# First feed-forward: the attention sum's shift by one token moved from TensorE to the sync queue's transfers

## The reference, cut to what matters

```python
def shift_token(t):                      # the second half of the channels comes from the token before
    t1, t2 = jnp.split(t, 2, axis=-1)
    t2 = jnp.pad(t2, ((0, 0), (1, 0), (0, 0)))[:, :-1]
    return jnp.concatenate([t1, t2], axis=-1)

def _layer(x, ...):
    ...                                  # local attention, 8 heads of 64, windows of 128 tokens, gives o
    x = x + o @ wo
    h = shift_token(x)
    mu = h.mean(-1, keepdims=True)
    var = h.var(-1, keepdims=True)
    h = (h - mu) / jnp.sqrt(var + 1e-05) * lg + lb
    h = h @ w1 + b1
    a, g = jnp.split(h, 2, axis=-1)
    h = a * jax.nn.gelu(g, approximate=False)
    x = x + h @ w2 + b2
    return x
```

## Time and profile before

| what | value |
|---|---|
| runs | 1794.33, 1794.79, 1800.66 us; median 1794.79 |
| the profiled execution's own time | 1796.17 us |
| its span in the trace | 1794.3 us |
| mean granted TensorE clock | 0.893 of full speed |
| busy PE / DVE / ACT / POOL | 83% / 60% / 41% / 24% of the span |
| the stage that the change is in | about 190 to 951 us |

### The profile page before, as it was taken

The page is one execution under the profiler, slowest core; times in us unless marked ns, Lnnn a source line. Parts: engine busy times, 40 slices in busy tenths (PEclk is TensorE's granted clock), DMA queues, the critical chain, the costliest instruction groups (busy, mean ns, idle before and its releaser), DMA issues. The chain is left out here.

```text
span 1794.3 us, 31159 instructions
## 1 busy us (share of the span) xinstructions
PE 1486.6 (83%) x9550; PEld 1171.4 (65%) x9551; DVE 1068.5 (60%) x2885; ACT 743.3 (41%) x1784; POOL 437.1 (24%) x469
## 2 busy tenths in 40 slices
PE   4985799999999999999998887299265699729992
PEld 3762477777777777777776565288142388618992
DVE  3326666666667777777765642677777566552223
ACT  1211555555556655555553211055266234202330
POOL 2102222222222222333321146111321100036321
PEclk9978899999999999999996798599675699859997
DMA  6001000000000000000003343610100000112104
GB/s 239 0 1 55 1 1 2 0 0 1 0 4 22 33 2 0 0 0 0 1 1 140 129 150 118 241 84 0 36 1 0 3 1 0 47 40 82 49 31 146
DMA packets 27138, 74.60 MB, mean 42 GB/s; under 512 B 6587, under 2 KB 11853, under 8 KB 25004
## 3 DMA queue, kind: packets, MB, share of 16 engines
q1 hardware_dynamic: 20236, 55.44, 8.3%
q0 software_dynamic: 6816, 18.14, 3.3%
HBM read 54.22 MB, written 20.88 MB: 42 GB/s over the span
## 5 line engine op out<-in xcount | busy, mean ns | idle before, releaser
L1124 PE MATMUL banks<-l_ffn_h2T,l_ffn_w 128*128 128x128 f32 (+1 forms) x1536 | 193.4, 277 | 0.0
L1124 PEld LDWEIGHTS banks<-l_ffn_h2T,l_ffn_w 128*128 128x128 f32 (+1 forms) x1536 | 178.6, 179 | 11.1 <-issue 5.7
L1041 PE MATMUL banks<-l_ffn_in_wqkv,l_ffn_hT 128*128 128x512 f32 x384 | 182.2, 612 | 0.8 <-ACT l_ffn_hT L1201 0.8
L1223 ACT ACTIVATE l_ffn_work<-l_ffn_work,l_ffn_att_bias 128x256 f32<-128x256 f32 x256 | 126.4, 495 | 76.9 <-DVE l_ffn_att_bias L1365 76.9
L1251 ACT ACTIVATE l_ffn_gate<-banks,l_ffn_layer_cols 128x128 f32<-128x128 f32 x192 | 59.9, 362 | 200.9 <-PE banks L1124 187.7
L1041 PEld LDWEIGHTS banks<-l_ffn_in_wqkv,l_ffn_hT 128*128 128x128 f32 x384 | 69.4, 194 | 75.8 <-issue 74.6
L265 POOL TENSOR_TENSOR rstd<-mean_var,neg_half 128x1 f32 x64 | 35.2, 550 | 338.3 <-DVE mean_var L258 338.3
L1132 PE MATMUL banks<-l_ffn_in_w,l_ffn_ff 128*128 128x256 f32 (+1 forms) x384 | 107.8, 396 | 0.0
L990 POOL TENSOR_TENSOR l_ffn_rden_wide<-l_ffn_att_rden,ones 128x512 f32<-128x512 f32 x32 | 33.3, 1040 | 273.1 <-DVE l_ffn_att_rden L1376 273.1
L2175 DVE COPY l_plan_c_all<-l_ffn_in_w 128x1024 f32 x39 | 31.4, 806 | 101.7 <-PE banks L2109 89.4
L1257 ACT ACT_TABLE_LOAD x68 | 87.2, 1283 | 1.2
(11 more groups left out here) (408 smaller groups left out, 3500.1 us busy)
## 6 DMA issues: line engine op xcount, KB each, us to landing
l_plan_rows<-l_plan_pairs SPq DMA_DIRECT2D x16, 512.0 KB, 8.3
l_ffn_in_w<-in_L_w SPq DMA_DIRECT2D x2, 4096.0 KB, 21.1
l_ffn_in_down<-in_L_down SPq DMA_DIRECT2D x1, 4096.0 KB, 14.4
l_plan_pairs<-l_plan_rows SPq DMA_DIRECT2D x4, 1024.0 KB, 7.0
l_plan_table<-l_plan_rows SPq DMA_DIRECT2D x8, 512.0 KB, 2.8
l_ffn_in_wqkv<-in_L_wqkv SPq DMA_DIRECT2D x1, 3072.0 KB, 12.1
l_ffn_w<-in_L_w SPq DMA_DIRECT2D x2, 1364.0 KB, 7.3
x_res<-in_x SPq DMA_DIRECT2D x4, 512.0 KB, 5.4
```

The costliest lines, as they stand in the source:

```text
L1041: mm = pe.matmul(ps[:, (Q, K, V)[n], :], hT[:, m.b, m.odd, ch, 1 - ch:P + 1 - ch], wqkv[:, bass.ds(m.layer, 1), ch, n * INNER:(n + 1) * IN ...
L1124: mm = pe.matmul(ps[0:FW[j], HIDDEN[pair], to:to + P], w1[:, ch, at:at + FW[j]], h2T[:, ch, m.b, :], start=(j % 2, n, ch) == (0, 0, 0), st ...
L1223: ex = nc.scalar.activation(work[:, m.b, slot, :], work[:, m.b, slot, :], ACT.Exp, bias=bias[:, m.b, slot:slot + 1], scale=-1.0, accum_out ...
```

## The change: what it does

`shifted` and its two products leave TensorE, and the two 128x128 matrices that it used are no longer loaded. In their place SyncE runs a step per item: it waits for y1 of the item and issues two transfers inside SBUF, each of the upper 128 channels in f32: one of 127 rows (partitions 0 to 126 to partitions 1 to 127), one of a single row (partition 127 of the tile before to partition 0). Both add 16 to the new semaphore `row_moved`, so that an item is done at 32. VectorE reads the shifted half from the new SBUF tile `moved` instead of PSUM. In VectorE's step, `shifted_stats` is split: `own_stats` stays, `moved_stats` stands after `take_y(after)`, and `normalise_h2` stands after `gated(old, 2)`. The two loads of the second layer are woven into SyncE's steps. LIFT, the offset of all semaphore counts, goes from 16 to 128.

```diff
-LIFT = 16
+LIFT = 128
...
-        self.shift = sb("shift", [P, 2, P])
...
+        moved = sb("moved", [P, BATCH, D - P])
...
             @block.sync
             def _(sp):
-                with sp.Fori(1, LAYERS) as layer:
-                    first = layer * HALF
-                    sp.wait_ge(s.rot_ready.sem, s.rot_ready.at(first, 0))
+                def move_row(m):
+                    sp.wait_ge(s.y1_ready.sem, s.y1_ready.at(m.turn, m.k))
+                    sp.dma_start(moved[1:P, m.b, :], y1[0:P - 1, m.b, m.odd, P:D]).then_inc(s.row_moved.sem, 16)
+                    sp.dma_start(moved[0:1, m.b, :], y1[P - 1:P, m.b, 1 - m.odd, P:D]).then_inc(s.row_moved.sem, 16)
...
+                def step(old, now, new, after):
+                    if now and new and new.opens and new.q == 0:
+                        next_rotation(new.layer)
+                    if now:
+                        move_row(now)
+                    if old and now and now.opens and now.q == 0:
+                        next_up(now.layer)
...
-                def shifted(m):
-                    pe.wait_ge(s.y1_ready.sem, s.y1_ready.at(m.turn, m.k))
-                    pe.matmul(ps[:, SHIFTED, D:D + P], shift[:, 0, :], y1[:, m.b, m.odd, P:D], start=True, stop=False)
-                    pe.matmul(ps[:, SHIFTED, D:D + P], shift[:, 1, :], y1[:, m.b, 1 - m.odd, P:D], start=False, stop=True)\
-                      .then_inc(s.shift_psum.sem, 1)
...
                     if old:
                         ffn_up(old, 1)
-                    if now:
-                        shifted(now)
-                    if old:
                         ffn_up(old, 2)
...
-                def shifted_stats(m):
+                def own_stats(m):
                     v.wait_ge(s.y1_ready.sem, s.y1_ready.at(m.turn, m.k))
                     v.bn_stats(bn2[:, m.b, 0, :], y1[:, m.b, m.odd, 0:P])
-                    v.wait_ge(s.shift_psum.sem, s.shift_psum.at(m.turn, m.k))
-                    dve.link(v.bn_stats(bn2[:, m.b, 1, :], ps[:, SHIFTED, D:D + P]))
+
+                def moved_stats(m):
+                    v.wait_ge(s.row_moved.sem, s.row_moved.at(m.turn, MOVED * m.k))
+                    dve.link(v.bn_stats(bn2[:, m.b, 1, :], moved[:, m.b, :]))
...
-                    v.tensor_scalar(h2[:, m.b, P:D], ps[:, SHIFTED, D:D + P], mv2[:, m.b, 0:1], rstd2[:, m.b:m.b + 1], ALU.subtract, ALU.mult)\
+                    v.tensor_scalar(h2[:, m.b, P:D], moved[:, m.b, :], mv2[:, m.b, 0:1], rstd2[:, m.b:m.b + 1], ALU.subtract, ALU.mult)\
...
                     if now:
                         add_attention(now)
-                        shifted_stats(now)
+                        own_stats(now)
                     if old:
                         gated(old, 1)
                     if after:
                         take_y(after)
                     if now:
-                        normalise_h2(now)
+                        moved_stats(now)
                     if old:
                         gated(old, 2)
+                    if now:
+                        normalise_h2(now)
                     if old and old.closes and old.q > 0:
                         stats_of(old.i, old.q - 1)
```

More of the change, by code:

```diff
@@ L126, in __init__ @@
         self.y1_ready = new("y1_ready")
-        self.shift_psum = new("shift_psum")
+        self.row_moved = new("row_moved")
         self.shift_var = new("shift_var")
@@ L213, in build @@
         e.s, e.dma_sem = Signals(new), sem
-        e.chain = {n: Chain(sem(f"{n}_order")) for n in ("dve", "act", "pool", "pe")}
+        e.chain = {n: Chain(sem(f"{n}_order")) for n in ("dve", "act", "pool", "pe", "sp")}
         e.loaded = sem("loaded")
@@ L405, in __init__ @@
         self.qk_scale = sb("qk_scale", [P, LAYERS, 2, 2, DH])
-        self.shift = sb("shift", [P, 2, P])
         self.mask32 = sb("mask32", [P, 3, 2 * P])
         super().__init__(e, "l0_ffn", ((self.all_cols, "L0_cols"), (self.all_b2, "L0_b2"), (self.qk_scale, "L0_qk_scale"),
-                         (self.shift, "shift"), (self.mask32, "mask"), (self.wqkv, "L0_wqkv"), (self.wo, "L0_wo"), (self.w2, "L0_w2")))
+                         (self.mask32, "mask"), (self.wqkv, "L0_wqkv"), (self.wo, "L0_wo"), (self.w2, "L0_w2")))
 class L0Xattn(Ahead):
@@ L822 @@
 HUGE = 3e38
+MOVED = 32
 def l0_ffn(e, ffn):
@@ L832, in l0_ffn @@
         sb = memory(e, ctx, "l0_ffn")
-        wqkv, wo, w2, all_cols, all_b2, qk_scale, shift, mask32 = (ffn.wqkv, ffn.wo, ffn.w2, ffn.all_cols, ffn.all_b2, ffn.qk_scale, ffn.shift, ffn.mask32)
+        wqkv, wo, w2, all_cols, all_b2, qk_scale, mask32 = (ffn.wqkv, ffn.wo, ffn.w2, ffn.all_cols, ffn.all_b2, ffn.qk_scale, ffn.mask32)
         y = sb("y", [P, ALL_TILES, D])
@@ L893, in l0_ffn @@
                 s.rot_ready, s.qkT_psum, s.qT_ready, s.kT_ready, s.rden_ready, s.rden_wide, s.mixed_psum, s.mix_ready, s.mixT_psum,
-                s.mixT_ready, s.out_psum, s.y1_ready, s.shift_psum, s.shift_var, s.shift_rstd, s.h2_ready, s.h2T_psum,
+                s.mixT_ready, s.out_psum, s.y1_ready, s.shift_var, s.shift_rstd, s.h2_ready, s.h2T_psum,
                 s.h2T_ready, s.y1b_ready, s.ffn_out, s.y_done)
@@ L900, in l0_ffn @@
         begin(4 * FPAIRS, s.hid_psum, s.gate_ready, s.ff_ready)
+        begin(4 * MOVED, s.row_moved)
         class Item:
@@ L913, in l0_ffn @@
         Q_T, K_T = 0, 1
-        SCORES, RDEN_T, MIXED, OUT, SHIFTED, H2_T = 2, 2, 3, 4, 4, 5
+        SCORES, RDEN_T, MIXED, OUT, H2_T = 2, 2, 3, 4, 5
         V, HIDDEN, DOWN, Y_T = 6, (6, 7, 6), 7, 3
@@ L958, in _, with next_rotation, next_up, first @@
             def _(sp):
-                with sp.Fori(1, LAYERS) as layer:
-                    first = layer * HALF
-                    sp.wait_ge(s.rot_ready.sem, s.rot_ready.at(first, 0))
+                def move_row(m):
+                    sp.wait_ge(s.y1_ready.sem, s.y1_ready.at(m.turn, m.k))
+                    sp.dma_start(moved[1:P, m.b, :], y1[0:P - 1, m.b, m.odd, P:D]).then_inc(s.row_moved.sem, 16)
+                    sp.dma_start(moved[0:1, m.b, :], y1[P - 1:P, m.b, 1 - m.odd, P:D]).then_inc(s.row_moved.sem, 16)
+                def next_rotation(layer):
+                    sp.wait_ge(s.rot_ready.sem, s.rot_ready.at(layer * HALF, 0))
                     sp.dma_start(rot[:], d["rotary"]).then_inc(rot_loaded, 16)
-                    sp.wait_ge(s.hid_psum.sem, s.hid_psum.at(first, 0))
+                def next_up(layer):
+                    sp.wait_ge(s.hid_psum.sem, s.hid_psum.at(layer * HALF, 0))
                     sp.dma_start(w1[:], d["L0_w1"][bass.ds(layer, 1)].rearrange("l p c n -> (l p) c n"))\
                       .then_inc(w1_loaded, 16)
+                def first(new):
+                    pass
+                def step(old, now, new, after):
[5 more added lines that the diff above has]
+                        next_up(now.layer)
+                layers(sp, e.chain["sp"], lambda layer: None, first, step)
             @block.gpsimd
@@ L1385, in add_attention @@
                     v.wait_ge(s.out_psum.sem, s.out_psum.at(m.turn, m.k))
-                    v.wait_ge(s.shift_psum.sem, s.shift_psum.at(m.turn, m.k - 2))
+                    v.wait_ge(s.h2_ready.sem, s.h2_ready.at(m.turn, m.k - 2))
                     v.wait_ge(s.y1b_ready.sem, s.y1b_ready.at(m.turn, m.k - 2))
                     if m.opens and m.q == 0:
-                        v.wait_ge(s.shift_psum.sem, s.shift_psum.at(m.turn, m.k - 1))
+                        v.wait_ge(s.row_moved.sem, s.row_moved.at(m.turn, MOVED * (m.k - 1)))
                         v.wait_ge(s.y1b_ready.sem, s.y1b_ready.at(m.turn, m.k - 1))
@@ L1480, in _ @@
                 layers(v, dve, lambda layer: None, first, step)
-        end(turns, *four, s.scores_psum, s.probs_ready, s.probsT_psum, s.bias_ready, s.pT_act, s.pT_dve, s.hid_psum, s.gate_ready, s.ff_ready)
+        end(turns, *four, s.row_moved, s.scores_psum, s.probs_ready, s.probsT_psum, s.bias_ready, s.pT_act, s.pT_dve, s.hid_psum, s.gate_ready, s.ff_ready)
         end(HALF, s.ln_var, s.ln_rstd)
```

## The result

The changed kernel takes 1851.8 us (median of 4 runs, 1848.6 to 1852.4) beside 1795.5 us for the kernel before on the same chip: 1.030 times as long, 95% interval 1.028 to 1.032. The forecast was 1858 us, with 1808 to 1930 as its range.

What follows compares the result with a forecast made beforehand. PE's order of work was taken to bound the first feed-forward stage. Waits for the rows summed 23.7 + 5.9 + 26.2 + 4.2 + 2.5 = 62.5 us onto 1796.2, giving 1858.7, stated as 1858 us, range 1808 to 1930.

Steps and rivals of the forecast that it cites:

- The landing: Transfer of 127 rows inside SBUF: all on one engine, 5.3 us from issue; each us of landing is 32 us of total.
- the bounds 1.8 and 7.2: Landing of the row transfer: 1.8 us if dealt out over 16 engines, 7.2 us on one engine at 46 ns a row.
- the wait on VectorE: DVE before `moved_stats`, each step of the first feed-forward stage: stands still 2.5 us until the rows land.
- the wait on PE: PE before h2's transposes or, in the last layer, the scores: waits 1.9 us (1.48 + 0.44), with DVE as releaser.
- The first layer's items: First layer and the step that crosses: h2 late, 1.48 us a step, 16 steps, 23.7 us.
- the 24.5: Sign against the prediction: same landing with a step shorter than 24.5 would mean a slack read as used up was not.
- The last layer: Last layer: 4 steps at +1.48 us, 5.9 us; 10 steps with `stats_of` before `copy_kT` at +2.62 us, 26.2 us.
- Both ends: First and last item of the stage: +4.2 us to the scores of the first, +2.5 us at the last.
- a slower granted clock: Sign against the prediction: PE's clock below 1.00 in the stage because PE pauses, adding to each product; not in the sum.
- The loads of the second layer: Rotary table and w1 on SP, now behind row moves: delayed under 2 us, needed some 10 us later, cost nothing.
- Rival B: Rows dealt out over engines, landing in 1.8 us; k late by 0.2 us in 10 steps; 5.7 us gained, 1790.5 us; chance 0.10.
- C's 14 us: Rival C: as B, but k isn't late and every item gains; 14 us less, 1782 us; chance 0.05.

Runs made afterwards that it cites:

- the run with `copy_kT` first: The changed kernel with `copy_kT` ahead of `stats_of` in the last layer: 1847.0 us, 1.027 of the kernel before.
- the run with 128 rows: The changed kernel with one transfer an item of all 128 rows straight down, no shift and no single row: 1785.8 us, 0.993 of before.
- run with 127 rows alone: The changed kernel without the single-row transfer, partition 0 of the shifted half staying zero: 1844.8 us, 1.026 of before.
- the run with 112 and 15 rows: The changed kernel with its 127 rows cut into transfers of 112 and 15, the single row mostly issued before the wait for y1: 1787.3 us, 0.994 of before.

## Why the prediction was right

The mechanism was right: the rows go one after another, VectorE waits for them, PE waits for VectorE, and in the last layer k comes late. The size, 62.5 us forecast against 55 measured, hides errors in both directions.

- *The landing*, on which the sum hung: 5.3 us plus 0.1 for SP, 5.40 after y1. Measured 5.39. The choice between the bounds 1.8 and 7.2 was right for the reason given, and the row that priced it (29 ns a packet) holds inside SBUF as well, where 28 ns were measured. That it fits to the hundredth is luck: SP took 0.03 us in place of 0.1, the 127 rows 5.15 in place of 5.3, and the single row, which the sum put at nothing, added 0.21. The Trainium skill's rule on how many engines a transfer takes (DMA: Bandwidth & Descriptors, "Why a DMA increments its semaphore by 16 and not by 1") agrees with the five large counts tried: 128 and 112 rows fast, 127, 113 and 97 slow. The same page of the Trainium skill gives an engine some 27 GiB/s ("Specifications"); by an estimate from that figure the rows would have taken 2.2 us, where 127 x 28 ns = 3.6 us was measured, so these rows of 512 B didn't reach it.
- *What bounds and what doesn't*: the wait on VectorE is 2.6 us a step, as forecast (2.5); the wait on PE 1.26 where 1.9 stood. The first layer's items were to be 1.48 us longer and are 1.13 on the mean of items 3 to 16, mostly 1.01 (24.30 against 23.29). That is under the 24.5 at which the prediction said that a slack had been misread. There was none; stretches were shorter than read. The largest is that from the rows to h2, 2.23 us by the earlier trace rows and 2.00 here (292.41 to 294.41): POOL's L1016 takes 0.56 us in place of 0.71, and L1422 0.34 in place of 0.41. I had written that reading SBUF changes hundredths; the larger part was POOL's time, which I took over from another neighbourhood. y1 also comes 0.16 us sooner after PE begins to load the h2 of the item before. And 1.26 us of wait less 0.44 of products is 0.82, not 1.01: before, h2's first product starts 0.17 us before the end of the product ahead of it (732.58 against 731.72 + 1.03, below), and after the wait it doesn't.
- *The last layer*: I forecast 2.62 us in 10 steps for `stats_of` ahead of k; the usual one is 1.53 longer (24.82 against 23.29), at the turn of a loop 1.1 (25.48 against 24.36), and three are longer for the clock (last section). The mechanism stands (10 waits of PE for k, and the run with `copy_kT` first). Of the 1.09 us too many in the usual one, 0.46 lie in L1435, 0.62 us of the 2.11 of the earlier trace rows, which here is 0.16 (L1449 above); 0.25 are those of the first layer, from y1 to h2; and some 0.4 are the scores themselves, 16 products that before stand 2.41 us around the last product of `ffn_down` (733.34 to 735.75, below) and run through in 2.00 after the wait for k. All 15 steps with the last layer's items, the crossing among them: 33.6 us forecast, 24.8 measured.

Timeline of before, further rows of the step of the earlier trace rows:

```profile
731.72 1.03 PE L1132 MATMUL banks<-l_ffn_in_w,l_ffn_ff 128*128 128x256 f32 x4
731.74 0.72 POOL L1002 TENSOR_TENSOR l_ffn_y1b<-l_ffn_y1b,x_res 128x256 f32<-128x256 f32 x1 [0.20 <-POOL l_ffn_y1b L999]
731.86 0.62 DVE L1435 TENSOR_TENSOR mean_var<-mv,zero_eps 128x2 f32 x1
...
732.58 0.38 PE L1109 MATMUL banks<-ident,l_ffn_h 128*128 128x128 f32 x2
...
733.66 2.09 PE L1064 MATMUL banks<-l_ffn_kT,l_ffn_qT 64*128 64x256 f32 x15
```

- *Both ends*: first item 4.2 forecast, 5.9 measured to h2, of which 1.2 were there before y1; the last 2.5 against 3.4; the second item 1.5 against 3.9 us. That one is a cost that the sum lacked and the text named as what would make it wrong, a slower granted clock (below).
- *The loads of the second layer*, put at nothing: the rotary table and w1 are issued while rows are on their way, and in these two items the rows come 5.97 and 5.67 us after y1 in place of the usual 5.4, 0.9 us together.

Sum of the items: 5.9 + 3.9 + 15.8 (14 items) + 24.8 + 3.4 = 53.8 us against 62.5. The steps of the first layer were forecast 4.9 us too dear and those of the last 8.8, and 5.0 us at the ends were missing. So the total is nearer than its parts, and that is luck too. Rival B's item, 22.85 us, is that of the run with 128 rows to the hundredth (22.84), and its weak point was right as a worry and wrong in size: k isn't late there, so the floor is C's 14 us and not B's 5.7.

## What to carry to other kernels

Before a product is replaced by a transfer between partitions, ask how the number of partitions divides: a shift by one leaves 127 rows, and here 127 or 113 rows of 512 B take about 5 us where 128 or 112 take 1.8 or 1.9. Cut such a count into parts that divide well, issue the part whose source is old early, and compare the landing with the time at which the consumer gets there and not with zero. And price a wait at the engine that bounds: VectorE's 88 us of waiting were 55 us of kernel time.

## What the runs showed of the hardware that was not expected

The clock of TensorE after an idle stretch. In the first item of the change PE waits 5.63 us for h2, and what follows runs slower than in the earlier trace rows (scores 2.00 us there, 3.79 here). Timeline of PE, and below it the busy times of two stretches (the number before the last two is the granted clock):

```profile
218.69 0.69 PE L1124 MATMUL banks<-ident,l_ffn_h 128*128 128x128 f32 x2 [5.63 <-DVE l_ffn_h L1422]
219.99 3.79 PE L1085 MATMUL banks<-l_ffn_kT,l_ffn_qT 64*128 64x256 f32 x16 [0.61 <-issue]
223.70 4.62 PE L1062 MATMUL banks<-l_ffn_in_wqkv,l_ffn_hT 128*128 128x512 f32 x8
```

```profile
218.50:224.00 5.50, 4.70 (x19) 3.32 (x20) 3.23 (x15) 1.82 (x7) 1.79 (x2) 0.50 0.00 0
224.00:230.00 6.00, 6.00 (x25) 3.48 (x25) 2.88 (x13) 4.48 (x16) 0.25 (x1) 0.87 0.01 4
```

0.50 is the lower of the two levels, 1.2 GHz. Scores and q/k products together take 2.7 us more than before (3.79 + 4.62 against 2.00 + 3.70); with the 1.0 to 1.2 us of the other items this makes the second item's 3.9. The steps' waits of 1.3 us leave the clock at 1.00 between 240 and 560 us, but in the last layer, where PE waits for h2 and then for k, it falls in 3 of 10 such items, for some us each:

```profile
719.00:724.00 5.00, 4.77 (x20) 3.24 (x20) 4.04 (x20) 1.42 (x5) 2.59 (x5) 0.66 0.00 0
```

The scores in that stretch (L1085 at 719.92) take 3.24 us where the usual is 2.00; at 795.68 they take 3.63 and at 921.49 3.42. The three items that follow are the longest of the layer, 26.5 us, where 24.3 to 25.5 are usual. In the run with `copy_kT` first PE has the same waits for h2 and none for k behind them, and its clock stays up:

```profile
240.00:980.00 740.00, 691.22 (x4789) 532.99 (x4788) 494.21 (x1496) 406.45 (x1083) 182.46 (x177) 1.00 0.02 7
```

The run with 127 rows alone, which has the 10 waits for k too, shows such falls as well (0.98 in its last layer). Each of these is one profiled execution.

An issue on SP is not one price: 0.46 us for 128 rows, 0.59 for 127, and with two in a row 0.62 and 0.94 us, where the two issues of the earlier trace rows took 0.90 together. It decided nothing here, but three issues in a row, as the run with 112 and 15 rows has them where the second layer starts, took 1.98 us (582.72 to 584.70).

And an instruction of VectorE on 128x2 elements can take four times as long beside GpSimd. In the trace of before L1435 takes 0.61 to 0.63 us in the 10 places where POOL's L1002, a sum of two tiles of 128x256, has started some 0.1 us earlier, and 0.16 in its other 6. There it ends within 0.03 us of L1002 (731.86 + 0.62 against 731.74 + 0.72). In the change L1449 never meets such a sum at its start and takes 0.16 throughout; L1005, which is longer (1.64 us) but works on 128x8, is still running when it starts in 10 places and doesn't hold it. No run was made to try this alone.
